# Local attention: the band mask added by VectorE instead of by mask products on TensorE

## What is computed

```python
WINDOW = 32; HEADS = 16; DIM_HEAD = 64; DEPTH = 6      # n = 512 tokens, nw = 16 windows
bk2, bv2 = look(bk), look(bv)                          # keys of the window before, and of its own: 64
mask = (it < jb) | (it > jb + w) | (jb == -1)
sim = jnp.einsum('bhwie,bhwje->bhwij', bq, bk2) * QK_SCALE
sim = jnp.where(mask, -jnp.finfo(sim.dtype).max, sim)
attn = jax.nn.softmax(sim, -1)
out = jnp.einsum('bhwij,bhwje->bhwie', attn, bv2)

for i in range(DEPTH):
    x = attn_layer(shift_tokens(x), Wqkv[i], q_scale[i], k_scale[i], Wo[i]) + x
    x = ffn_layer(shift_tokens(x), ln_g[i], ln_b[i], W1[i], b1[i], W2[i], b2[i]) + x
```

## Time and profile before

| | |
|---|---|
| median of 3 runs | 4428.97 us (4423.1 to 4429.79) |
| the profiled execution | 4426.65 us |
| its span in the profile | 4424.9 us |
| busy in the span: TensorE, VectorE, ScalarE, GpSimd | 97%, 74%, 59%, 49% |
| mean granted TensorE clock | 0.991 of full speed |
| `pass1`: first projection starts at | 1181.22 us |
| one trip of `pass1` | some 66 us |

### The profile page before, as it was taken

How to read it: one execution, slowest core, us unless ns; L and a number is a source line. 1 busy time by engine, 2 the same in 40 slices (tenths; PEclk the granted TensorE clock), 3 DMA queues, 4 the chain that set the end, 5 groups by cost and what they waited for, 6 DMA issues and landing times.

```text
span 4424.9 us, 159360 instructions
## 1 busy us (share of the span) xinstructions
PE 4276.1 (97%) x68360; PEld 2558.4 (58%) x68360; DVE 3267.2 (74%) x5759; ACT 2617.6 (59%) x5346; POOL 2168.4 (49%) x1986
## 2 busy tenths in 40 slices
PE   8999999999799999999999999999999999999998
PEld 5555555555356656656666656656656656656655
DVE  5666666565577878877887877877877777877875
ACT  5544555455356666666666666666666666666664
POOL 0000000000266766766766766766766766766763
PEclk9999999999899999999999999999999999999998
DMA  1000000000111112111121111211122111221112
GB/s 45 4 8 6 8 6 6 6 8 4 46 47 50 48 46 68 50 50 49 49 69 52 48 46 50 69 49 50 48 60 58 44 51 46 62 60 49 49 47 67
DMA packets 141403, 185.95 MB, mean 42 GB/s; under 512 B 32870, under 2 KB 63652, under 8 KB 140708
## 3 DMA queue, kind: packets, MB, share of 16 engines
q1 hardware_dynamic: 140708, 175.76, 14.6%
HBM read 26.76 MB, written 4.19 MB: 7 GB/s over the span
## 4 chain that ended last, share of the span: by engine, by line
PE 70%; issue 1%; DVE 1%; POOL 1%; DMA 0%; SPq 0%; ACT 0%; DVEq 0%; POOLq 0%; ACTq 0%
PE psum L1599 23%; PE psum L1540 10%; PE psum L1604 8%; PE psum L1616 8%; PE psum L1525 6%; PE psum L1637 6%; PE psum L1609 4%; PE psum L1642 3%; PE psum L1562 1%; PE psum L1622 1%; PE psum L1632 0%; POOL qk L1489 0%; POOL cs L1480 0%; DVE cs L1779 0%; DVE rots L1743 0%
## 5 line engine op out<-in xcount | busy, mean ns | idle before, releaser
L1480 POOL TENSOR_TENSOR cs<-cs 128x512 f32<-128x512 f32 x768 | 975.6, 1276 | 545.2 <-DVE cs L1779 526.6
L1599 PE MATMUL psum<-wqkv,xw 128*128 128x512 f32 x2304 | 1184.1, 613 | 10.1 <-DMA wqkv<-in_wqkv 10.1
L1779 DVE TENSOR_TENSOR cs<-psum,rots 128x1024 f32<-128x1024 f32 x768 | 935.1, 1218 | 244.8 <-PE psum L1599 237.0
L1489 POOL TENSOR_TENSOR qk<-cs,rn 128x512 f32<-128x512 f32 x768 | 776.4, 1042 | 407.9 <-ACT rn L1663 407.9
L1676 ACT ACTIVATE sq<-psum 128x512 f32<-128x512 f32 x768 | 459.6, 598 | 538.7 <-DVE cs L1779 176.1
L1508 POOL MEMSET tiled<- 128x128 bf16 x1 | 0.2, 204 | 1170.0 <-POOLq L590 1170.0
L1736 DVE TENSOR_REDUCE ss<-sq 128x8 f32<-128x512 f32 x768 | 519.7, 677 | 11.7
L1540 PEld LDWEIGHTS psum<-pT,vw 64*64 64x64 f32 x18432 | 401.0, 135 | 203.4 <-issue 203.1
L1599 PEld LDWEIGHTS psum<-wqkv,xw 128*128 128x128 f32 x2304 | 371.0, 191 | 179.7 <-issue 139.9
L1540 PE MATMUL psum<-pT,vw 64*64 64x32 f32 x18432 | 446.5, 222 | 22.8 <-issue 18.0
L1604 PEld LDWEIGHTS psum<-ident,qk 128*128 128x128 f32 x3072 | 352.6, 141 | 168.9 <-issue 158.6
(11 more groups left out here) (198 smaller groups left out, 6639.0 us busy)
## 6 DMA issues: line engine op xcount, KB each, us to landing
vw<-vl SPq DMA_DIRECT2D x768, 128.0 KB, 2.4
vw<-vl SPq DMA_DIRECT2D x672, 64.0 KB, 2.0
wqkv<-in_wqkv SPq DMA_DIRECT2D x36, 256.0 KB, 4.2
wol<-in_wol SPq DMA_DIRECT2D x6, 512.0 KB, 3.8
xin<-in_x SPq DMA_DIRECT2D x9, 256.0 KB, 2.9
xr<-in_x SPq DMA_DIRECT2D x8, 256.0 KB, 3.0
sums<-sumout SPq DMA_DIRECT2D x8, 256.0 KB, 2.3
cs<-sums SPq DMA_DIRECT2D x8, 256.0 KB, 4.6
```

The lines of the kernel that those rows point to most:

```text
L1480: summed_rot.done(nc.gpsimd.tensor_tensor(own, own, halves(cs[:, t % 2, j, 1, :])[:, :, ::-1, :], ALU.add), at)
L1489: rotated.done(nc.gpsimd.tensor_tensor(qk[:, j, :].rearrange("p (h c) -> p h c", c=EL), cs[:, t % 2, j, 0, :].rearrange("p (h c) -> p h c" ...
L1599: last = nc.tensor.matmul(ps[:, :], xw[:, t * P:(t + 1) * P], wqkv[:, col:col + BANK], start=True, stop=True)
L1779: parts.done(V.tensor_tensor(cs[:, t % 2, j, :, :].rearrange("p i (h c) -> p i h c", c=EL), twice, by_head, ALU.mult), at)
```

## The change

The mask products are gone, and with them `tiled` and its making. The first products of a bank now have `start=True`. When VectorE reads the scores from the bank, it adds the band mask and writes the result to `probl` in SBUF; maximum and subtraction then work on `probl`. A bank of scores has a new reader, this addition (`masked` in place of `centered`). The mask itself is laid out by query row, where it was laid out for the products. The line numbers of the diff are its own; in the new file the addition is L1777, the maximum L1782, the subtraction L1736, the products with the values L1538.

```diff
--- before.py
+++ after.py
@@ -217,8 +217,7 @@
 
 
 PARITIES = 2
-PADS, TILES = 4, 10
-MADE = PADS + TILES
+MADE = 4
 WK = 2 * WIN
 MOVES = [6, 8, 8, 8]
 
@@ -1230,7 +1229,6 @@
         self.xw = sb("xw", [P, N + 1])
         self.xm = sb("xm", [P, N + 1])
         self.least = sb("least", [P, 1])
-        self.tiled = sb("tiled", [P, P], BF16)
         self.sq = sb("sq", [P, 2, BANK])
         self.ss, self.ssc = sb("ss", [P, 2, 2 * HL]), sb("ssc", [P, 2, 2 * HL])
         self.lns, self.rn = sb("lns", [P, 2 * HL]), sb("rn", [P, 2, 2 * HL])
@@ -1261,7 +1259,7 @@
 
     wqkv, wol, w1l, w2l, b1l, lng, lnb, b2l = buf.wqkv, buf.wol, buf.w1l, buf.w2l, buf.b1l, buf.lng, buf.lnb, buf.b2l
     qks, rot, rots, xw, xm, sq, ss, ssc = buf.qks, buf.rot, buf.rots, buf.xw, buf.xm, buf.sq, buf.ss, buf.ssc
-    least, tiled = buf.least, buf.tiled
+    least = buf.least
     lns, rn, cs, qk, qTl, kTl, vl, vw = buf.lns, buf.rn, buf.cs, buf.qk, buf.qTl, buf.kTl, buf.vl, buf.vw
     negmaxl, probl, pT, suml, rs, oTl, stats = buf.negmaxl, buf.probl, buf.pT, buf.suml, buf.rs, buf.oTl, buf.stats
     mv, lnv, rstd, x2, x2T, gel, hf, qkv_loaded = buf.mv, buf.lnv, buf.rstd, buf.x2, buf.x2T, buf.gel, buf.hf, buf.qkv_loaded
@@ -1294,6 +1292,7 @@
     parts = steps("parts", place("qk"))
     summed = steps("summed", place("qk"))
     clamped = steps("clamped", lambda key: key[1] if key[0] == "n" else None)
+    masked = steps("maskedl", place("s"))
     maxed = steps("maxedl", place("s"))
     centered = steps("centered", place("s"))
     totalled = steps("totalled", place("s"))
@@ -1315,7 +1314,7 @@
     link, rlink, passed = sem("linkl"), sem("rlinkl"), sh.passed
     finished = steps("finished", place("f"))
     sums_loaded = [sem(f"sums_loaded{k}") for k in range(2)]
-    out_stored, zeroed = sem("out_stored"), sem("zeroed")
+    out_stored = sem("out_stored")
     sums, outs = (cs[:, k, :, :, :].rearrange("p j i (a d) -> p (j i a) d", d=D).rearrange("p (s t) d -> p s t d", t=T)
                   for k in range(2))
 
@@ -1330,7 +1329,7 @@
         if kind == "t":
             return [(tcopied, at)]
         if kind == "s":
-            return [(centered, at)]
+            return [(masked, at)]
         if kind == "pt":
             return [(turned, at)]
         if kind == "o":
@@ -1505,7 +1504,6 @@
                         r = rs[:, t % 2, 4 * k:4 * k + 4, :].rearrange("p c two -> p (c two)")
                         weighed.done(nc.gpsimd.tensor_tensor(p, p, r.unsqueeze(2).to_broadcast([P, 8, WK]), ALU.mult), (t, k))
 
-            nc.gpsimd.memset(tiled[:, :], 0.0).then_inc(zeroed, 1)
             fetched.done(nc.gpsimd.tensor_copy(xw[:, :], state[:, 0, :]), "first")
             nc.gpsimd.memset(least[:, :], 1e-24).then_inc(made, 1)
             nc.gpsimd.memset(xm[:, :], 0.0).then_inc(made, 1)
@@ -1526,7 +1524,7 @@
                                 banks[p][WIN * w:WIN * w + WIN, c * WK:(c + 1) * WK],
                                 qTl[rows, t % 2, c, WIN * w:WIN * w + WIN],
                                 kTl[rows, c, t * P + WIN * w:t * P + WIN * w + WK],
-                                start=False, stop=True, skip_group_check=True)
+                                start=True, stop=True, skip_group_check=True)
                 return last
 
             def output_half(t, banks, blocks):
@@ -1555,13 +1553,6 @@
                         settle(pe, passed)
                     banks = [psum[b] for b in ring.take_both(pe, it, [("s", t, p) for p in range(PARITIES)], [turned_k])]
                     settle(pe, passed)
-                    for w in range(4):
-                        own = slice(WIN * w, WIN * w + WIN)
-                        for p in range(PARITIES):
-                            rows = slice(64 * p, 64 * p + 64)
-                            nc.tensor.matmul(banks[p][own, :].rearrange("p (c k) -> p c k", k=WK), tiled[rows, own],
-                                             maskw[rows, min(t, 1), :].unsqueeze(1).to_broadcast([64, PAIRSL, WK]),
-                                             start=True, stop=False, skip_group_check=True)
                     score_half(t, banks, range(PAIRSL // 2))
                     return
                 if kind == "s":
@@ -1716,11 +1707,6 @@
             V = nc.vector
             V.memset(kTl[:, :, 0:WIN], 0.0).then_inc(made, 1)
             V.memset(vw[:, 0, 0, :], 0.0).then_inc(made, 1)
-            dve.wait_ge(zeroed, 1)
-            for a in range(4):
-                rows = slice(WIN * a, WIN * a + WIN)
-                for w in range(4 if a % 2 == 0 else 1):
-                    V.tensor_copy(tiled[rows, WIN * w:WIN * w + WIN], ident[rows, rows]).then_inc(made, 1)
             dve.wait_ge(made, MADE)
             chain = Chain(dve, link, 0, once=True)
             HALF = D // 2
@@ -1746,9 +1732,8 @@
             def center(it, t, p):
 
                 maxed.wait(dve, it, (t, p))
-                centered.done(V.tensor_tensor(
-                    probl[:, t % 2, :, p, :], psum[ring.bank(it, ("s", t, p))][:, :].rearrange("p (c k) -> p c k", k=WK),
-                    negmaxl[:, t % 2, :, p].unsqueeze(2).to_broadcast([P, PAIRSL, WK]), ALU.add), (t, p))
+                x = probl[:, t % 2, :, p, :]
+                centered.done(V.tensor_tensor(x, x, negmaxl[:, t % 2, :, p].unsqueeze(2).to_broadcast([P, PAIRSL, WK]), ALU.add), (t, p))
 
             def total(it, t, p):
 
@@ -1788,9 +1773,14 @@
                     finished.done(V.tensor_tensor(outs[:, at[0], :, own], ps[:, 0:4 * 64].rearrange("p (t d) -> p t d", d=64),
                                                   sums[:, at[0], :, own], ALU.add), at)
                 elif kind == "s":
-                    maxed.done(V.tensor_reduce(negmaxl[:, t % 2, :, at[1]], ps[:, :].rearrange("p (c k) -> p c k", k=WK),
-                                               AX.X, ALU.max, negate=True), at)
+                    x = probl[:, t % 2, :, at[1], :]
+                    masked.done(V.tensor_tensor(x, ps[:, :].rearrange("p (c k) -> p c k", k=WK),
+                                                maskw[:, min(t, 1), :].unsqueeze(1).to_broadcast([P, PAIRSL, WK]), ALU.add), at)
                     if at[1] == 1:
+                        for p in range(PARITIES):
+                            masked.wait(dve, it, (t, p))
+                            maxed.done(V.tensor_reduce(negmaxl[:, t % 2, :, p], probl[:, t % 2, :, p, :], AX.X, ALU.max, negate=True),
+                                       (t, p))
                         for p in range(PARITIES):
                             center(it, t, p)
                 elif kind == "y":
@@ -1873,7 +1863,7 @@
     r, own = np.arange(WK)[None, :], q % WIN
     later = np.where((own <= r) & (r <= own + WIN), 0.0, NEG)
     unpaired = np.where((r < WIN) & (later == 0.0), NEG, 0.0)
-    return causal.astype(np.float32), np.stack([np.where(q % WK < WIN, later, one) for one in (unpaired, 0.0)], 1).astype(np.float32)
+    return causal.astype(np.float32), np.stack([np.where(q < WIN, later + one, later) for one in (unpaired, 0.0)], 1).astype(np.float32)
 
 
 def kernel(**inputs):
```

## The result

| | before | changed |
|---|---|---|
| median, same chip | 4426.03 us (4418.9 to 4429.79, 4 runs) | 4566.24 us (4551.82 to 4566.68, 4 runs) |
| ratio, 95% interval | | 1.0309 [1.0287, 1.0331] |
| span in the profile | 4424.9 us | 4564.7 us |
| mean granted TensorE clock | 0.991 | 0.981 |
| mean length of trips 1 to 45 | 66.42 us | 69.38 us |

The change costs 140 us. The forecast was 4500 us with a range up to 4524: the sign was right, the size about half. A trip became 2.96 us longer, where +1.55 had been worked out.

What follows compares the result with a forecast made beforehand. TensorE, busy 497.01 of 500 us, was taken as the bound, so late operands add directly. Trips of +1.82 and +1.02 us, two to one, gave 1.55 x 47 = +73 on 4426.65: 4500 us, range 4433 to 4524.

Steps and rivals of the forecast that it cites:

- four bursts: Mask products on TensorE, one burst per token tile: removing them returns 0.23 us each, 0.92 us a trip.
- wait of `oa.2`: Tile 3: TensorE waits for ScalarE's copy of `v.0.1`, delayed by VectorE; `oa.2` moves by +1.21 us net of one burst.
- `t.1.3` and `pt.0.0`: Two TensorE waits after tile 0's late subtractions: +1.30 us a trip, 0.50 in about one trip in three.
- the sum: Terms per trip added: +1.82 us, or +1.02 in the second kind, two to one: 1.55 us, times 47 = +73 us.
- gelu in a layer's first trip: Behind tile 2, gelu comes 1.2 us later, less than the room there except in a layer's first trip; nothing added.
- The stage: VectorE's work per token tile grows by two instructions, 1.20 us; masked addition 681 ns, reduction 678, subtraction 691 before any delay.
- The collision: VectorE's subtraction with two SBUF operands waits for the running GpSimd instruction and ends about 0.54 us behind it.
- the first rival: Subtractions don't wait for GpSimd: `oa.2` moves 0.97 us, a trip +0.28 us, time 4440 us; chance 0.28.
- Tile 3: First subtraction meets GpSimd; the second ends at 2127.62 against 2126.41, so everything to `oa.2` moves +1.21 us.
- Tile 0: Subtractions meet GpSimd's four instructions and end 3.7 us later; `t.1.3` and `pt.0.0` wait, +1.30 us in such a trip.
- Tiles 1 and 2: Longer VectorE stage is covered by other TensorE work, GpSimd is idle there; each tile still returns 0.23 us.
- the third rival: Delays spread into the next trip and tile 3's squares: 2.1 us a trip, +99 us, time 4526 us; chance 0.10.

Runs made afterwards that it cites:

- the copy first: Changed kernel with ScalarE's copy of `v.0.1` placed ahead of tile 3's exponentials: 4503.46 us, ratio 1.0171.
- TensorE kept busy: Changed kernel with the transposes of `t.0.3` done three times, so TensorE works through most of the wait before `oa.2`: 4543.07 us, ratio 1.026.
- a few steps moved: Changed kernel with copies of `v.0.1` and `pt.2.1` ahead of tile 3's exponentials, `pt.2.1` behind tile 3's scores, `pt.0.0` two steps later: 4484.57 us.
- `pt.3.0` moved too: The run with a few steps moved, and `pt.3.0` also placed behind `sa.0` and `n.1`: 4484.48 us.
- joined halves: Changed kernel with each first half of a tile's scores and outputs moved down to its second: 4497.59 us; same edit on the kernel before: 4352.48 us.
- the order with room: Halves joined, at least 1.7 us of other steps between groups of small products: changed kernel 4437.06 us, kernel before 4389.34 us.
- the order with four groups of small products in a row: Changed kernel, halves joined, second new order with `sa.0`, `s.0.0`, `oa.3`, `o.3.0` adjacent and gelu behind all exponentials: 4545.5 us, ratio 1.0255.

## Why the prediction was wrong

In us per trip, the prediction's terms and what the trace of after shows:

| term | predicted | measured |
|---|---|---|
| four bursts | -0.92 | -0.94 |
| wait of `oa.2` | +1.44 | +1.61 |
| `t.1.3` and `pt.0.0` | +1.03 (mean) | +0.92 |
| the four steps behind `oa.2`, lower clock | not in the sum | +0.81 |
| gaps inside `s.1.0` | not in the sum | +0.32 |
| gelu in a layer's first trip | 0 | +0.12 |
| `t.3.0` once, 3.2 us in the second trip | 0 | +0.07 |
| all (measured: with 0.05 in other steps) | +1.55 | +2.96 |

**The burst.** Right: 0.23 said, 0.19 with nothing else changed. **The stage.** Right: 1.20 us a tile; masked addition 684 ns, reduction 675, both within 3 ns of the rows taken. The rule of the Trainium skill, VectorE: DVE Perf Modes, section on the TRN2 errata, that I set aside for the earlier trace rows stays set aside: reading SBUF in place of PSUM made the reduction 10 ns shorter, not 65. **The collision.** Right in kind and place, from ten instances of L1743: long subtractions only at tiles 3 and 0. The mean of 893 ns, and 680 without the SBUF pair, rule out the first rival. (Its working says that tile 0 adds 2.19 us to VectorE; the 0.8 and 0.2 us of room that it gives go with 1.94.) **Tile 3.** Right: the copy of `v.0.1` ends, and `oa.2` starts 0.09 us later; 0.17 us more than worked out. **Tile 0.** Right within 0.12 us. **Tiles 1 and 2.** Nearly right: their subtractions meet no GpSimd; but the delay of gelu that I called smaller than the room "but in a layer's first trip" costs 1.0 us in five trips, and I had not added it. The wait of 3.2 us in the second trip is for GpSimd's product ahead of `t.3.0`, and was not foreseen.

**The step that failed is the sum.** Up to there it holds: the three terms come to 1.59 us against 1.55. It took the time of TensorE to be its work plus its waits, at one clock. The earlier trace rows shows a clock of 1.00 in a kernel in which TensorE hardly ever stops; that says nothing about a kernel in which it stops 1.7 us in every trip. The four steps behind the stop take 0.81 us a trip more than before, where the sum has nothing, and the run in which TensorE was kept busy through the wait gives the net price, 23 us. The second part is the 0.32 us inside `s.1.0`: 14 gaps of 0.9 us, in trips 3, 6, 9 and so on, each 1.1 to 1.6 us behind the landing of an instruction fetch. The kernel before has such gaps too, 22 us in all, and I didn't read them. Why they grow there is open: the kernel with no bursts has the same number of instructions and 1.7 us of gaps at this place, and the one with the scores kept in PSUM next to none; in those two `t.1.3` and `pt.0.0` don't wait, in the changed kernel and in the two variants with the gaps (the copy first, TensorE kept busy; 12 to 13 us) they do. That is a correlation and no more, and a weak one: with a few steps moved `t.1.3` still waits 0.37 us, and the gaps there are 3 us. My range ended at 4524 because the third rival was built from the same terms at their worst; a mechanism that is not in any term was in no bound either.

## What to carry to other kernels

Work taken from a full engine returns what it occupied there (here 0.19 us a burst), while the queue that gets it passes its delay on to whoever waits behind it; so the price is read at the first instruction of the full engine that hangs on the longer queue. When a change gives a busy TensorE its first regular stop, put a price on the clock behind that stop, beside the stop itself. Look for time inside groups that wait for nothing: adjacent short groups of one kind were cheaper than split ones (0.20 us a joint here), but with four of them in a row TensorE stopped 179 us inside its steps, each time behind a fetch of instructions.

## What the runs showed that I had not expected

- A stop of 1.7 us in a trip of 70 us was enough for 14 stretches at half clock in 47 trips, while one of 1.0 us (the copy first) gave none. The length of the stop alone does not decide it: stops of 1.5 us ahead of `sa.0` (`pt.3.0` moved too) gave none either, and the changed kernel with joined halves, with stops of 1.4 us ahead of `oa.2`, has 15 stretches, of which seven begin within 4 us behind such a stop. What does decide it is open.
- A VectorE subtraction with two SBUF inputs that met a GpSimd instruction ended 0.5 to 0.6 us behind that instruction's end, in all 134 cases, and 44 GpSimd instructions took 1.49 us instead of 1.04.
- TensorE stops inside groups that wait for nothing, 1.2 to 1.6 us behind the landing of a 16 KB instruction fetch: 22 us in the kernel before, 76 and 104 us in the kernels before and changed in the order with room, 179 us in the order with four groups of small products in a row.
- A change between large and small products costs TensorE about 0.1 us each way: joining eight pairs of groups made the kernel before 1.7% faster.
